# Wide attention: values behind the ring on TensorE, exponentials behind the ring copies on ScalarE

## The chip, the cores and the metric

The kernel runs on one core of a Trainium2 chip. The metric is the device time of one execution in microseconds (us); several runs give a median. The core has a matrix engine (TensorE, PE in the profile, its weight loads PEld), a vector engine (VectorE, DVE), a scalar engine (ScalarE, ACT), GpSimd (POOL) and an engine that mostly issues DMAs (SyncE, SP). Each works through its own instructions strictly in the order in which they are written; only semaphores tie one engine to another.

## What is computed

The whole program is a decoder of four layers with attention, cross attention and feed forward parts. The change touches one part, the cross attention of layer 1, over 8 batch entries, 256 queries each, and a context of 1601 rows with one learned null row added (1602 keys), 16 heads of 64:

```python
q = _split_heads(jnp.einsum('bnd,df->bnf', x, Wq))
kv = jnp.einsum('bmc,cf->bmf', context, Wkv)
k, v = jnp.split(kv, 2, axis=-1)
...
k = jnp.concatenate((nk, k), axis=-2)
v = jnp.concatenate((nv, v), axis=-2)
q = q * scale
sim = jnp.einsum('bhid,bhjd->bhij', q, k)
attn = jax.nn.softmax(sim, axis=-1)
out = jnp.einsum('bhij,bhjd->bhid', attn, v)
out = out.transpose(0, 2, 1, 3).reshape(b, -1, INNER)
out = jnp.einsum('bnf,fd->bnd', out, Wout)
```

A layer norm follows. All of it is float32.

## The kernel before

The stage (`stage4`) works in **units**: a unit is one batch entry and a pair of heads, 64 units in all. The two heads of a unit lie in the upper and the lower 64 partitions, so their score matmuls use the two halves of TensorE's rows, and their value matmuls the two halves of its columns. The 1602 keys of a unit are cut into 13 tiles of up to 128 (the last has 66), the tiles into 7 **slots** (six of two tiles, the last of one). The main loop of every engine takes two slots in a **step**. Since a unit has 7 slots, the pattern repeats after 14 slots, which are seven steps and two units.

A slot x passes these stations:

- scores (TensorE, L2870): keys by queries into one of two pairs of PSUM banks, keys on the partitions;
- score copy (ScalarE, L2942): PSUM to the SBUF tile `sc`;
- maxima (VectorE, L3027 and L3030): a running elementwise maximum over the tiles of the unit;
- ten slots later (`LAG - 2`) the subtraction of the maximum in place (VectorE, L3008) and the exponential in place (ScalarE, L2948); GpSimd adds the exponentials up tile by tile (L2992);
- twelve slots later (`LAG`) the values (TensorE, L2884), accumulated over the unit in PSUM;
- fourteen slots after the last slot of a unit the **sums** (TensorE, L2925: ones times the added exponentials), then on VectorE the reciprocal (L3040) and the multiplication (L3043).

Between these, TensorE does what the following units need, in a **ring** of two PSUM banks. `ring_of(s)` lists the keys of a step in their order: `q` (L2837), `k` in four chunks (L2846) and `v` (L2854) are projections; `turn` (L2904) transposes the maxima of a unit, whose reduce over keys VectorE makes (L3016); `bcast` (L2911) spreads the result over the partitions; `out` (L2919) is the output projection, once in 8 units. A key can start only when the key two places before it has been copied out of its bank (`ring_bank`, which waits for `n - 2`). The copies are ScalarE's (L2958 for q, L2964 for k, L2970 for v, L2975 for bcast), that of `turn` is VectorE's reduce and that of `out` a VectorE copy.

The order by hand in a step is, before the change:

- TensorE: scores, values, ring, sums;
- ScalarE: score copies, exponentials, ring copies;
- VectorE (unchanged): subtractions, reduce of a turn, maxima, copy of `out`, reciprocal and multiplication;
- GpSimd (unchanged): the adds.

A turn of unit u-1 is in the step with slot 7u+1, the sums of a unit in the step with a slot 7m-1, so the step with sums is followed at once by a step with a turn. The scores of a new unit wait for the copies of its q and of its last k chunk. The values of a step wait for exponentials that ScalarE made in the step before.

Of the kernel before, what the change touches and what calls it, by code (L numbers as in the profile page):

```python
# [16 lines left out]
ACT = mybir.ActivationFunctionType  # L17
# [2756 lines left out]
def stage4(env):  # L2774
    ps, branch, x_feat, ident = env.ps, env.branch, env.x_feat, env.ident
    with ExitStack() as ctx:
        st = Stage(env, ctx, "wide")
        plan = WideSlots()
# [46 lines left out]
        @block.tensor  # L2825
        def _(pe):
            def ring_bank(key):
                n = plan.index[key]
                if n >= 2:
                    wait_copied(pe, plan.order[n - 2])  # L2830
                return n % 2

            def project(key):
                if key[0] == "q":
                    u = key[1]
                    bank = ring_bank(key)
                    return pe.matmul(ps[:, bank, 0:S], W("wq")[:, u % HP * P:u % HP * P + P],  # L2837
                                     x_feat[:, u // HP * S:u // HP * S + S], start=True, stop=True)
                if key[0] == "k":
                    u, c = key[1:]  # L2840
                    if u % HP == 0 and c == 0:
                        pe.wait_ge(ctx_loaded, 16 * (u // HP + 1))
                    bank = ring_bank(key)
                    lo, hi = plan.chunks[c]
                    for half in range(2):
                        ins = pe.matmul(ps[:, bank, 0:hi - lo],  # L2846
                                        W("wk")[:, half * INNER + u % HP * P:half * INNER + u % HP * P + P],
                                        ctxT[:, u // HP % 2, half, lo:hi], start=(half == 0), stop=(half == 1))
                    return ins
                g, t = key[1:]  # L2850
                bank = ring_bank(key)
                c0, rows = t * P, min(P, SC - t * P)
                for half in range(2):
                    ins = pe.matmul(ps[0:rows, bank, 0:2 * P], ctxT[:, g // 4 % 2, half, c0:c0 + rows],  # L2854
                                    W("wv")[:, half * INNER + g % 4 * 2 * P:half * INNER + g % 4 * 2 * P + 2 * P],
                                    start=(half == 0), stop=(half == 1))
                return ins

            def scores(s, u, k):
                if k == 0:  # L2860
                    wait_copied(pe, ("q", u))
                    wait_copied(pe, ("k", u, 3))
                if s >= 2:
                    pe.wait_ge(s_copied, s - 1)
                    before, step = plan.unit(s, 2)
                    pe.wait_ge(max_done, len(tiles) * before + plan.tiles_of(step)[-1] + 1)
                for t in plan.tiles_of(k):
                    c0, rows = tiles[t]
                    for e in range(2):
                        ins = pe.matmul(ps[0:rows, 2 + 2 * (s % 2) + e, t % 2 * S:(t % 2 + 1) * S],  # L2870
                                        kT[e * HW:(e + 1) * HW, u % 2, c0:c0 + rows],
                                        q[e * HW:(e + 1) * HW, u % 2, :], start=True, stop=True)
                ins.then_inc(st_ready, 1)

            def values(s, u, k):
                if k == 0 and u >= 2:
                    pe.wait_ge(normed, u - 1)
                wait_copied(pe, ("v", u // 2, plan.tiles_of(k)[-1]))
                pe.wait_ge(exp_done, s + 1)
                for t in plan.tiles_of(k):  # L2880
                    rows = tiles[t][1]
                    for e in range(2):
                        c0 = u % 2 * P + e * HW
                        ins = pe.matmul(ps[e * HW:(e + 1) * HW, 6 + u % 2, 0:S], v[0:rows, u // 2 % 2, t, c0:c0 + HW],  # L2884
                                        sc[0:rows, u % 2, t, e * S:(e + 1) * S], start=(t == 0), stop=(t == last_tile))
                ins.then_inc(pv_done, 1)

            pe.wait_ge(w_loaded, 16)
            pe.wait_ge(null_moved, 32)
            pe.wait_ge(null_k_ready, 1)  # L2890
            pe.wait_ge(ones_ready, 1)
            for s in range(plan.first, plan.end, 2):
                for slot in plan.pair(s):
                    scores(*slot)
                for slot in plan.pair(s, plan.LAG):
                    values(*slot)
                for key in plan.ring_of(s):
                    if key[0] in ("q", "k", "v"):
                        project(key).then_inc(ring_ready, 1)
                    elif key[0] == "turn":  # L2900
                        pe.wait_ge(max_done, len(tiles) * (key[1] + 1))
                        bank = ring_bank(key)
                        for j in range(4):
                            ins = pe.transpose(ps[:, bank, j * P:(j + 1) * P], top[:, key[1] % 2, j * P:(j + 1) * P],  # L2904
                                               ident[:, :])
                        ins.then_inc(ring_ready, 1)
                    elif key[0] == "bcast":
                        wait_copied(pe, ("turn", key[1]))
                        bank = ring_bank(key)
                        for j in range(4):  # L2910
                            ins = pe.matmul(ps[:, bank, j * P:(j + 1) * P], mx[:, j:j + 1].to_broadcast([P, P]),  # L2911
                                            ident[:, :], start=True, stop=True)
                        ins.then_inc(ring_ready, 1)
                    else:
                        pe.wait_ge(normed, HP * (key[1] + 1))
                        bank = ring_bank(key)
                        for qt in range(2):
                            for p in range(HP):
                                ins = pe.matmul(ps[:, bank, qt * D:(qt + 1) * D], oT[:, p, qt * P:(qt + 1) * P],  # L2919
                                                W("wout")[:, p * D:(p + 1) * D], start=(p == 0), stop=(p == HP - 1))  # L2920
                        ins.then_inc(ring_ready, 1)
                for u in plan.ended(s, plan.LAG + 2):
                    pe.wait_ge(added, last_tile * (u + 1))
                    for e in range(2):
                        ins = pe.matmul(ps[e * HW:(e + 1) * HW, 6 + u % 2, S:2 * S], ones[:, :],  # L2925
                                        acc[:, u % 2, e * S:(e + 1) * S], start=True, stop=True)
                    ins.then_inc(sums_done, 1)

        @block.scalar
        def _(act):  # L2930
            act.wait_ge(null_moved, 32)
            for s in range(plan.first, plan.end, 2):
                for x, u, k in plan.pair(s):
# [6 lines left out]
                    src = ps[0:rows, 2 + 2 * (x % 2):4 + 2 * (x % 2), 0:n * S].rearrange("p e (j q) -> p e j q", j=n)  # L2940
                    dst = sc[0:rows, u % 2, 2 * k:2 * k + n, :].rearrange("p j (e q) -> p e j q", e=2)
                    act.activation(dst, src, ACT.Copy).then_inc(s_copied, 1)  # L2942
                for x, u, k in plan.pair(s, plan.LAG - 2):
                    n = len(plan.tiles_of(k))
                    rows = tiles[2 * k][1]
                    act.wait_ge(sub_done, x + 1)
                    e = sc[0:rows, u % 2, 2 * k:2 * k + n, :]
                    act.activation(e, e, ACT.Exp).then_inc(exp_done, 1)  # L2948
                for key in plan.ring_of(s):
                    if key not in plan.act_count:  # L2950
                        continue
# [7 lines left out]
                    elif key[0] == "k":  # L2959
                        u, c = key[1:]  # L2960
                        lo, hi = plan.chunks[c]
                        if u >= 2:
                            act.wait_ge(st_ready, plan.STEPS * (u - 1))
                        act.activation(kT[:, u % 2, lo:hi], ps[:, bank, 0:hi - lo], ACT.Copy).then_inc(ring_act, 1)  # L2964
                    elif key[0] == "v":
                        g, t = key[1:]
                        rows = min(P, SC - t * P)
                        if g >= 2:
                            act.wait_ge(pv_done, plan.STEPS * (2 * g - 3) + t // 2 + 1)
                        act.activation(v[0:rows, g % 2, t, :], ps[0:rows, bank, 0:2 * P], ACT.Copy).then_inc(ring_act, 1)  # L2970
                    else:
                        u = key[1]
                        if u >= 2:
                            act.wait_ge(sub_done, plan.STEPS * (u - 1))
                        act.activation(mb[:, u % 2, :], ps[:, bank, :], ACT.Copy).then_inc(ring_act, 1)  # L2975

        @block.gpsimd
        def _(pool):
# [1463 lines left out]
```

## Time and profile before

| | us |
|---|---|
| median of 3 runs | 5105.78 |
| lowest, highest | 5103.46, 5122.11 |
| the profiled execution, time | 5113.21 |
| the profiled execution, span of its trace | 5111.4 |
| TensorE busy, whole span | 4084.8 (80%) |
| VectorE, ScalarE, GpSimd busy | 3495.8, 2508.5, 1378.3 |

The stage lies from about 890 to 2708 us of the span. A row of a view by stretches reads: the stretch, its length, then the busy time (with the number of instructions) of PE, PEld, DVE, ACT and POOL, the clock granted to TensorE as a share of 2.4 GHz, the share of the DMA engines and GB/s. A row of the list of waits reads: who waited, for whom, the time in total, how often, the longest; all in us. A row of the timeline reads: start in us, busy time in us of the instructions that were merged into the row, engine, line, operation, output and input, shape, number; in brackets the idle time before it and who ended it. A matmul of float32 shows as two records, and a busy time in such a row runs to the end of the last matmul, which overlaps the next row; so the time that a group costs is read from start to start.

### The profile page before, as it was taken

The numbers are of one execution on the slowest core, as the hardware profiler recorded it, in microseconds if no ns is written. First come the engines' busy times: TensorE is split into PE (matmuls) and PEld (weight loads), VectorE is DVE, ScalarE is ACT, GpSimd is POOL, SyncE is SP. The second block draws the span as 40 slices with busy tenths as digits, with TensorE's granted clock in tenths as the row PEclk, the third lists the DMA queues.
The fourth block names the chain that finished last, engine by engine and source line by source line (L and its number), as shares of the span: only waits on it lengthen the run. The fifth ranks groups of instructions, "written<-read, shape, count | busy, mean of one in ns | idle before, by whom it ended". The sixth has DMA issues, their size and how long they took to land. (4 is left out here: it accounts for less than half of the span.)

```text
span 5111.4 us, 77588 instructions
## 1 busy us (share of the span) xinstructions
PE 4084.8 (80%) x29250; PEld 2216.5 (43%) x29315; DVE 3495.8 (68%) x5424; ACT 2508.5 (49%) x3542; POOL 1378.3 (27%) x1033
## 2 busy tenths in 40 slices
PE   5740596999999999999995995866995768888872
PEld 3530234666666666666652332432443332222221
DVE  5379444677777777777784445766773648888867
ACT  2120142666666666666662223543563345776762
POOL 0000300566666666666665302000000100000000
PEclk5565698999999999999997997987997788999986
DMA  0010001000000000000003106316540333323200
GB/s 19 1 60 0 0 0 51 1 14 1 14 1 14 14 1 14 1 14 1 1 1 129 58 0 148 54 14 108 81 72 4 95 66 59 55 43 49 47 2 8
DMA packets 135604, 167.70 MB, mean 33 GB/s; under 512 B 19499, under 2 KB 108093, under 8 KB 134677
## 3 DMA queue, kind: packets, MB, share of 16 engines
q1 hardware_dynamic: 127540, 146.39, 14.1%
q0 software_dynamic: 6528, 16.42, 1.3%
q8 instruction: 231, 3.78, 0.3%
q14 instruction: 121, 0.98, 0.1%
q10 hardware_dynamic: 1184, 0.12, 0.0%
HBM read 125.31 MB, written 34.55 MB: 31 GB/s over the span
## 5 line engine op out<-in xcount | busy, mean ns | idle before, releaser
L2992 POOL TENSOR_TENSOR arena<-arena 128x512 f32<-128x512 f32 (+1 forms) x768 | 1131.8, 1475 | 692.2 <-ACT arena L2948 638.8
L2443 ACT ACTIVATE arena<-ps 128x1024 f32<-128x1024 f32 (+1 forms) x688 | 703.9, 1024 | 331.9 <-PE ps L2368 321.4
L2461 DVE TENSOR_REDUCE arena<-ps 128x2 f32<-128x826 f32 (+1 forms) x576 | 565.0, 981 | 183.6 <-PE ps L2314 175.1
L3008 DVE TENSOR_TENSOR arena<-arena 128x1024 f32<-128x1024 f32 (+1 forms) x448 | 645.9, 1480 | 13.8 <-ACT arena L2975 13.8
L3030 DVE TENSOR_TENSOR arena<-ps,arena 128x512 f32<-128x512 f32 (+1 forms) x768 | 530.3, 691 | 177.8 <-ACT arena L2942 144.4
L2314 PE MATMUL ps<-arena 48*128 48x413 bf16 (+3 forms) x1920 | 435.2, 333 | 135.0 <-DVE arena L2461 67.2
L2942 ACT ACTIVATE arena<-ps 128x1024 f32<-128x1024 f32 (+1 forms) x448 | 410.6, 961 | 204.8 <-PE ps L2870 194.3
L2854 PE MATMUL ps<-arena 128*128 128x256 f32 (+1 forms) x1664 | 444.1, 392 | 20.5 <-DVE arena L3016 19.2
L2948 ACT ACTIVATE arena<-arena 128x1024 f32<-128x1024 f32 (+1 forms) x448 | 424.9, 992 | 50.7 <-DVE arena L3008 48.2
L2387 PE MATMUL ps<-arena 128*9 128x256 f32 (+2 forms) x5504 | 435.3, 388 | 11.7 <-ACT arena L2431 8.0
L2870 PE MATMUL ps<-arena 64*128 64x256 f32 (+1 forms) x3328 | 427.3, 391 | 5.6 <-ACT arena L2964 1.3
L2884 PE MATMUL ps<-arena 128*64 128x256 f32 (+1 forms) x3328 | 412.7, 388 | 5.8 <-ACT arena L2948 5.8
L2846 PE MATMUL ps<-arena 128*128 128x400 f32 (+1 forms) x1024 | 400.1, 513 | 2.9 <-ACT arena L2970 2.8
L2870 PEld LDWEIGHTS ps<-arena 64*128 64x128 f32 (+1 forms) x3328 | 301.1, 182 | 149.7 <-issue 94.8
L2368 PE MATMUL ps<-arena 51*128 51x256 bf16 (+3 forms) x2752 | 349.1, 276 | 10.5 <-DMA arena<-arena 10.5
L2854 PEld LDWEIGHTS ps<-arena 128*128 128x128 f32 (+1 forms) x1664 | 282.4, 185 | 154.5 <-issue 61.4
L2314 PEld LDWEIGHTS ps<-arena 48*128 48x128 bf16 (+1 forms) x1920 | 127.5, 96 | 461.1 <-DVE arena L2461 230.4
L2884 PEld LDWEIGHTS ps<-arena 128*64 128x64 f32 (+1 forms) x3328 | 220.7, 137 | 171.5 <-issue 84.5
L2262 POOL COPY arena<-arena 128x1536 f32<-128x1536 f32 (+2 forms) x40 | 30.0, 782 | 932.2 <-DMA arena<-arena 605.5
L2964 ACT ACTIVATE arena<-ps 128x400 f32<-128x400 f32 (+1 forms) x256 | 129.5, 506 | 256.7 <-PE ps L2846 256.7
L2846 PEld LDWEIGHTS ps<-arena 128*128 128x128 f32 x1024 | 182.6, 190 | 127.1 <-ACT arena L2970 14.3
L2368 PEld LDWEIGHTS ps<-arena 51*128 51x128 bf16 (+3 forms) x2752 | 170.4, 98 | 108.1 <-issue 55.0
(645 smaller groups left out, 5796.0 us busy)
## 6 DMA issues: line engine op xcount, KB each, us to landing
arena<-ctx_parts SPq DMA_DIRECT2D x96, 200.1 KB
arena<-ctx_parts SPq DMA_DIRECT2D x192, 100.1 KB
arena<-in_ctx_feat SPq DMA_DIRECT2D x8, 1601.0 KB, 6.5
arena<-in_ctx SPq DMA_DIRECT2D x16, 768.0 KB
arena<-diff_att_stack SPq DMA_DIRECT2D x60, 192.0 KB
ctx_parts<-arena SPq DMA_DIRECT2D x24, 400.2 KB, 3.7
arena<-in_w SPq DMA_DIRECT2D x1, 6416.0 KB, 18.6
arena<-in_ctx_feat SPq DMA_DIRECT2D x8, 800.5 KB
```

The source lines that it names most:

```text
L2314: return pe.matmul(self.ps[:, bank, c0:c0 + hi - lo], self.qst[r0:r1, ring, self.slot(g, h), q * P:(q + 1) * P], self.kst[r0:r1, ring, sel ...
L2368: ins = pe.matmul(self.ps[0:rows, 2 * (u % 2) + k % 2, k // 2 * S:(k // 2 + 1) * S], self.kst[r0:r1, ring, self.slot(g, k), c:c + rows], s ...
L2387: ins = pe.matmul(self.ps[32 * k:32 * k + self.hd + 1, 6, 0:S], self.vh[0:rows, b % 2, t, h0 + k, :], self.prob[0:rows, u % 3, k % 2 * 2 * ...
L2443: act.activation(self.prob[0:rows, u % 3, :], self.ps[0:rows, 2 * (u % 2):2 * (u % 2) + 2, :].rearrange("p n c -> p (n c)"), ACT.Exp).then ...
L2461: ins = dve.tensor_reduce(dst[:, :, j // 2], self.ps[:, 4:6, 0:hi - lo], AX.X, ALU.max)
L2846: ins = pe.matmul(ps[:, bank, 0:hi - lo], W("wk")[:, half * INNER + u % HP * P:half * INNER + u % HP * P + P], ctxT[:, u // HP % 2, half, ...
L2854: ins = pe.matmul(ps[0:rows, bank, 0:2 * P], ctxT[:, g // 4 % 2, half, c0:c0 + rows], W("wv")[:, half * INNER + g % 4 * 2 * P:half * INNER ...
L2870: ins = pe.matmul(ps[0:rows, 2 + 2 * (s % 2) + e, t % 2 * S:(t % 2 + 1) * S], kT[e * HW:(e + 1) * HW, u % 2, c0:c0 + rows], q[e * HW:(e + ...
L2884: ins = pe.matmul(ps[e * HW:(e + 1) * HW, 6 + u % 2, 0:S], v[0:rows, u // 2 % 2, t, c0:c0 + HW], sc[0:rows, u % 2, t, e * S:(e + 1) * S], ...
L2992: pool.tensor_tensor(acc[0:rows, u % 2, :], before, sc[0:rows, u % 2, t, :], ALU.add).then_inc(added, 1)
L3008: dve.tensor_tensor(e, e, mb[0:rows, u % 2, None, :].to_broadcast([rows, n, 2 * S]), ALU.subtract).then_inc(sub_done, 1)
L3030: ins = dve.tensor_tensor(most, got, most, ALU.max)
```

## The change

Two blocks move; nothing is added or removed, and no wait is changed. In TensorE's step `values` goes from between the scores and the ring to behind the ring, ahead of the sums. In ScalarE's step the exponentials go from between the score copies and the ring copies to the end.

```diff
             for s in range(plan.first, plan.end, 2):
                 for slot in plan.pair(s):
                     scores(*slot)
-                for slot in plan.pair(s, plan.LAG):
-                    values(*slot)
                 for key in plan.ring_of(s):
...
                         ins.then_inc(ring_ready, 1)
+                for slot in plan.pair(s, plan.LAG):
+                    values(*slot)
                 for u in plan.ended(s, plan.LAG + 2):
                     pe.wait_ge(added, last_tile * (u + 1))
...
                     act.activation(dst, src, ACT.Copy).then_inc(s_copied, 1)
-                for x, u, k in plan.pair(s, plan.LAG - 2):
-                    n = len(plan.tiles_of(k))
-                    rows = tiles[2 * k][1]
-                    act.wait_ge(sub_done, x + 1)
-                    e = sc[0:rows, u % 2, 2 * k:2 * k + n, :]
-                    act.activation(e, e, ACT.Exp).then_inc(exp_done, 1)
                 for key in plan.ring_of(s):
...
                         act.activation(mb[:, u % 2, :], ps[:, bank, :], ACT.Copy).then_inc(ring_act, 1)
+                for x, u, k in plan.pair(s, plan.LAG - 2):
+                    n = len(plan.tiles_of(k))
+                    rows = tiles[2 * k][1]
+                    act.wait_ge(sub_done, x + 1)
+                    e = sc[0:rows, u % 2, 2 * k:2 * k + n, :]
+                    act.activation(e, e, ACT.Exp).then_inc(exp_done, 1)
```

TensorE, in the step with a turn that follows a step with sums (the row L2925), before the change. Line numbers behind the moved block differ by two after it: L2904 becomes L2902, L2911 becomes L2909.

```order
L2925 MATMUL ps<-arena 64x256 x2
L2870 MATMUL ps<-arena 128x256 x8
L2884 MATMUL ps<-arena 64x256 x8
L2904 MATMUL ps<-ident,arena 128x128 x4
L2837 MATMUL ps<-x_feat,arena 128x256
L2854 MATMUL ps<-arena 128x256 x2
L2911 MATMUL ps<-ident,arena 128x128 x4
L2854 MATMUL ps<-arena 128x256 x2
L2846 MATMUL ps<-arena 128x401 x2
L2870 MATMUL ps<-arena 128x256 x8
```

The same place on TensorE after the change:

```order
L2884 MATMUL ps<-arena 64x256 x8
L2925 MATMUL ps<-arena 64x256 x2
L2870 MATMUL ps<-arena 128x256 x8
L2902 MATMUL ps<-ident,arena 128x128 x4
L2837 MATMUL ps<-x_feat,arena 128x256
L2854 MATMUL ps<-arena 128x256 x2
L2909 MATMUL ps<-ident,arena 128x128 x4
L2854 MATMUL ps<-arena 128x256 x2
L2846 MATMUL ps<-arena 128x401 x2
L2884 MATMUL ps<-arena 64x256 x8
L2870 MATMUL ps<-arena 128x256 x8
```

The values (L2884) have left the place between the scores (L2870) and the turn and stand at the end of the step; in the step before they now stand next to the sums (L2925).

ScalarE, in the same two steps, before the change:

```order
L2942 ACTIVATE arena<-ps 66x512
L2948 ACTIVATE arena<-arena 128x1024 x2
L2970 ACTIVATE arena<-ps 65x256
L2964 ACTIVATE arena<-ps 128x400
L2942 ACTIVATE arena<-ps 128x2x2x256 x2
L2948 ACTIVATE arena<-arena 128x1024 x2
L2958 ACTIVATE arena<-ps 128x256
```

ScalarE at the same place after the change (the exponential is L2975 now, the copy of v L2964, of k L2958, of q L2952):

```order
L2942 ACTIVATE arena<-ps 66x512
L2964 ACTIVATE arena<-ps 65x256
L2958 ACTIVATE arena<-ps 128x400
L2975 ACTIVATE arena<-arena 128x1024 x2
L2942 ACTIVATE arena<-ps 128x2x2x256 x2
L2952 ACTIVATE arena<-ps 128x256
```

The two exponentials have moved behind the copies of v and k of their step.

## Rows read from the trace of the kernel before

**Rows 1.** Busy times by stretch, middle of the stage.

```profile
1600.00:1800.00 200.00, 196.89 (x1202) 126.34 (x1198) 153.74 (x165) 128.69 (x190) 126.32 (x86) 1.00 0.03 9
```

**Rows 2.** List of waits, 880 to 2700 us.

```profile
PEld ps L2870 <- ACT arena L2964: 32.6, 64, 1.3
...
PE ps L2854 <- DVE arena L3016: 19.2, 32, 0.6
...
PEld ps L2846 <- ACT arena L2970: 14.3, 31, 3.2
```

**Rows 3.** Timeline of TensorE, steps G (from 1765.83) and A (from 1772.27).

```profile
1765.83 1.57 PE L2870 MATMUL ps<-arena 64*128 64x256 f32 x12
...
1771.56 0.65 PE L2925 MATMUL ps<-arena 128*64 128x256 f32 x4
1772.27 2.00 PE L2870 MATMUL ps<-arena 64*128 64x256 f32 x16
1774.19 1.95 PE L2884 MATMUL ps<-arena 128*64 128x256 f32 x16
1776.07 0.66 PE L2904 MATMUL ps<-ident,arena 128*128 128x128 f32 x4
...
1777.79 1.13 PE L2854 MATMUL ps<-arena 128*128 128x256 f32 x4 [0.63 <-DVE arena L3016]
...
1782.05 2.00 PE L2870 MATMUL ps<-arena 64*128 64x256 f32 x16
```

**Rows 4.** Timeline of TensorE, sums and then step E (from 1748.91).

```profile
1748.33 0.65 PE L2925 MATMUL ps<-arena 128*64 128x256 f32 x4
...
1748.91 2.00 PE L2870 MATMUL ps<-arena 64*128 64x256 f32 x16
...
1752.72 0.66 PE L2904 MATMUL ps<-ident,arena 128*128 128x128 f32 x4
...
1753.21 1.03 PE L2854 MATMUL ps<-arena 128*128 128x256 f32 x4
...
1754.25 1.58 PE L2846 MATMUL ps<-arena 128*128 128x401 f32 x4
...
1758.95 1.35 PE L2870 MATMUL ps<-arena 64*128 64x256 f32 x10
```

**Rows 5.** Timeline of VectorE, steps A and E, and other pairs of subtractions.

```profile
1751.16 1.84 DVE L3008 TENSOR_TENSOR arena<-arena 128x1024 f32<-128x1024 f32 x2
...
1757.39 2.43 DVE L3008 TENSOR_TENSOR arena<-arena 128x1024 f32<-128x1024 f32 x2 [0.44 <-ACT arena L2975]
...
1764.05 3.62 DVE L3008 TENSOR_TENSOR arena<-arena 128x1024 f32<-128x1024 f32 x2
...
1772.26 1.76 DVE L3040 RECIPROCAL arena<-ps 128x256 f32<-128x256 f32 x1 [1.98 <-PE ps L2925]
...
1774.39 2.75 DVE L3008 TENSOR_TENSOR arena<-arena 128x1024 f32<-128x1024 f32 x2
1777.06 0.68 DVE L3016 TENSOR_REDUCE arena<-ps 128x4 f32<-128x512 f32 x1
```

**Rows 6.** Timeline of ScalarE and GpSimd in step G.

```profile
1768.41 2.00 ACT L2948 ACTIVATE arena<-arena 128x1024 f32<-128x1024 f32 x2
...
1771.66 0.51 ACT L2964 ACTIVATE arena<-ps 128x400 f32<-128x400 f32 x1 [0.96 <-PE ps L2846]
...
1769.54 5.38 POOL L2992 TENSOR_TENSOR arena<-arena 128x512 f32<-128x512 f32 x4 [0.72 <-ACT arena L2948]
```

**Rows 7.** Stretches and timeline of TensorE, start and end of the stage.

```profile
926.00:927.00 1.00, 0.68 (x1) 0.50 (x2) 1.00 (x1) 0.55 (x3) 0.99 (x1) 0.50 0.00 0
...
926.33 3.04 PE L2846 MATMUL ps<-arena 128*128 128x400 f32 x4 [2.83 <-ACT arena L2970]
...
2669.60 2.08 PE L2911 MATMUL ps<-ident,arena 128*128 128x128 f32 x8 [4.88 <-DVE arena L3016]
...
2666.80:2673.60 6.80, 4.00 (x18) 3.03 (x20) 5.25 (x5) 3.23 (x4) 4.33 (x4) 0.50 0.01 2
```

## The prediction

> **What bounds the kernel now.** The change touches one stage of the program, the wide attention, so I looked first at the busy times by stretch. In 1600 to 1800 us TensorE is busy 196.89 of 200 us at a granted clock of 1.00, VectorE 153.7, ScalarE 128.7 and GpSimd 126.3 [rows 1]. TensorE is the bound, the others have 23 to 37% of slack, and any time in which TensorE waits is added to the kernel. Next I read the list of waits. TensorE waits for VectorE's reduce L3016 32 times, 19.2 us in all; the weight loads of the scores stand 32.6 us for the last key copy of a unit (L2964), 64 times, and 14.3 us for a value copy (L2970) [rows 2]. That is all there is to win: 0.3 to 0.5 us at a time.
>
> Then the timeline. The order of work repeats every 14 slots (two units, seven steps): 55.1 us. The two steps that hold a "turn" decide the case; I call them A and E. The reader should lay the rows of TensorE and of VectorE side by side.
>
> Step A begins with the scores at 1772.27. Scores take 1.92 us, values 1.88, then come the turn (1776.07), q and, at 1777.79, a v projection that had to wait 0.63 us for VectorE's reduce; the next step begins at 1782.05, so A lasts 9.78 us [rows 3]. Why is the reduce late? VectorE starts the reciprocal at 1772.26, because the sums of the step before were issued only at 1771.56, then the multiplication, then two subtractions (1774.39, 2.75 us), and only then the reduce at 1777.06 [rows 3, 5]. The reduce is tied to the sums and not to the turn: VectorE takes its work in order. With two ring banks, the second projection behind the turn can't start until the reduce has emptied the turn's bank.
>
> Step E begins at 1748.91: turn at +3.81 us, v at +4.30, k at +5.34, next step at +10.04 [rows 4]. VectorE's subtractions start at +2.25 and take 1.84 us [rows 5].
>
> **What the change moves.** It adds and removes no instruction; it costs only through order. (1) TensorE's values go from between scores and ring to behind the ring. (2) ScalarE's exponentials go from between score copies and ring copies to behind the ring copies.
>
> (1) In A and E the 1.9 us of values lay under VectorE's chain from reciprocal to reduce. That cover is taken away; the sums stay the last thing before the next scores, so the chain keeps its place. Queued behind TensorE's new wait are the rest of the ring, the values and all that follows; ScalarE's ring copies wait with it.
>
> (2) The exponentials end later in the step. Values use the exponentials of the step before, so these still have some 5 us; no wait there. But GpSimd adds what the exponentials deliver. In step G (before A) the exponentials run at 1768.41 and GpSimd's four adds at 1769.54 for 5.38 us, done at 1774.92, just as A's subtractions begin [rows 6]. G starts at 1765.83 [rows 3]. Its key copy stood at 1771.66 for 0.51 us [rows 6]; without the values (1.88) ahead of the projection it comes at 1769.8, and the exponentials follow it at 1770.3, 4.5 us into G instead of 2.6. The adds start 1.1 us after them, as now, at 5.6 of the 6.2 us that G then takes. GpSimd then works from A's start to A +5.4 or later, over the whole of A's subtractions. The same shift puts the adds of the step before E over E's.
>
> What subtractions cost beside GpSimd is in the trace: a pair takes 2.43 us with GpSimd idle (1757.39) and 3.62 us beside its adds (1764.05) [rows 5]. For A I take 3.62 for 2.75. E's pair is one full and one half tile: 3.62/2 for the full one and about 1.2 for the half one, an estimate, 3.0 for 1.84. Lower bound for both: as now.
>
> In the Trainium skill, "SBUF — State Buffer", section "SBUF: two separate sides", the port pair that VectorE and GpSimd share is an exclusive lock and the loser blocks for a whole instruction. By that rule each subtraction could wait out one add (5.38/4 = 1.35 us), a pair taking 2.43 + 2.7 = 5.1 us; the trace's pair beside adds took 3.62 [rows 5], so the measurement decides and the rule stays a rival.
>
> **Step A after.** Scores no longer wait for the key copy, so sums to scores is 0.58 (1748.33 to 1748.91, [rows 4]) instead of 0.71 (1771.56 to 1772.27, [rows 3]), and all of VectorE's chain shifts to +0.12: subtractions at 2.25, reduce at 2.25 + 3.62 - 0.08 = 5.79, v 0.73 later (as 1777.06 to 1777.79) at 6.52. TensorE is free at 1.93 + 0.5 (turn) + 0.5 (q, an estimate by the turn's) = 2.93: 3.6 us idle. From v to the end of A took 4.26 us; to this the values come: 6.52 + 4.26 + 1.93 = 12.71, against 9.78: **+2.93 us**.
>
> **Step E after.** Reduce ends at 2.25 + 3.0 + 0.6, k at 5.9; TensorE is free at 1.93 + 0.49 + 1.0 = 3.4: 2.5 us idle. k to the end took 4.70 (1754.25 to 1758.95): 5.9 + 4.70 + 1.93 = 12.5, against 10.04: **+2.5 us**. If subtractions stay as fast as now, A is +2.06 and E +1.43.
>
> **What comes back.** The last key copy of a unit is now under the values (two a period, 0.3 us each net of the change of tiling that stays), and a ring copy no longer stands behind two exponentials (0.2). Sum: **-0.7 us**. By [rows 2] it can't exceed (32.6 + 14.3)/31 = 1.5. The other steps have no new wait.
>
> Per period: 2.93 + 2.5 - 0.7 = +4.7 us. The reciprocal precedes the turn in 31 periods: **+147 us**.
>
> **The clock.** TensorE never idled in mid-stage; now it would idle 3.6 and 2.5 us per period. What follows such idling is in the same stage at its start: after 2.83 us of idle time the granted clock is 0.50 (926 to 927 us), which is 1.2 instead of 2.4 GHz, and the four matmuls of a k projection show 3.04 us where they show 1.58 at 1754.25 [rows 4, 7]: 1.4 us lost. At the stage's end the very chain of this prediction stands bare: few values left to cover the reduce, 4.88 us of idle time until 2669.60, and the clock at 0.50 for 6.8 us, 2666.8 to 2673.6 [rows 7]. So a fall costs from 1.4 us to half of 6.8, 3.4 us. For A I take 1.7 (nearest to the first row, a little more since its idle time is longer), for E 1.5 in two falls of three: 1.0. Together 2.7 x 31 = **+84 us**. Bounds: 0, and 2 x 3.4 x 31 = 211.
>
> On this the Trainium skill ("TensorE: Matmul & The Clock Gate", section "HAM oscillation — how this bites in real kernels") tells of a kernel whose matmuls restarted at half clock after each recurring wait. By that rule the 84 us belong in the sum; without it the sum would be 147. The rows at 926 us and 2667 us agree with it.
>
> One thing is won once: the wait at 926.33 stood behind the first exponentials and goes, 2.83 + 1.4 = 4 us.
>
> Sum: 147 + 84 - 4 = +227 us. The profiled execution had a span of 5111.4 us and took 5113.21; 5113 + 227 = 5340. It lies 7 us above the median of the runs (5105.78), so the forecast for the median is 5106 + 227 = **5333 us**, 4.4% slower.
>
> **The rivals.**
> - The clock holds. For it: most of the stage runs at 1.00 with small gaps. Against: both long gaps of this stage brought it down. 5106 + 147 - 4 = 5249. Chance 0.18.
> - GpSimd's adds don't fall on the subtractions. A +2.06, E +1.43, less 0.7: 2.79 x 31 = 86; with 1.4 us for a fall in A alone, 43 more: 5188 to 5231. Chance 0.09.
> - Half clock for the long spell, as at 2666.8, in both steps: 2 x (3.4 - 0.5 of idle time in it) = 5.8 instead of 2.7 a period: 5333 + 96 = 5429. Chance 0.05.
> - Subtractions blocked for a whole add each: 1.5 us more in A and as much in E, x 31 = 93: 5426. The rule is that of "SBUF — State Buffer" in the Trainium skill. Chance 0.03.
> - Faster. The mechanism is the key copy: scores of a new unit find it ready. Price -0.7 us a period, 22 us, and 4 at the start: 5080. It decides only if the reduce has ended by +2.9 us in A and +3.4 in E, when TensorE wants the bank; but the reciprocal (1.76 us) and the subtractions alone reach past +4. Chance 0.04.
> - Nothing within the noise: TensorE's losses met by gains, up to 1.5 us a period and half of A's loss. Chance 0.02.
>
> **How the numbers follow.** The forecast has 0.59. Its own range, with the bounds of the clock term and shorter subtractions, is 5270 to 5400. To hold 8 in 10 the range takes in the held clock and the upper end of the second rival: 5210 to 5400. Slower than by 0.5% (26 us, about what a measurement of this kernel can tell from no change) are all but the last two: 0.94; within 0.02; faster 0.04.
>
> **What would show it.** Waits of TensorE for the reduce should go from 19 us to some (3.6 + 2.5) x 31 = 190 us, 62 to 64 times; if they stay under 60 us the account of the cover is wrong. The wait of the scores for L2964's successor goes. A pair of subtractions behind a reciprocal lasts 3 us or more; if 2.4 to 2.8, the second rival holds. The granted clock of 1000 to 2600 us falls from 1.00 to some 0.9; if it stays, the first rival does. The stage's period goes from 55.1 to some 62.5 us. I would be wrong altogether if VectorE got its reciprocal done earlier, or if ScalarE's later exponentials held TensorE's values, which I price at nothing: cover is 5 us, and a step would lose what exceeds it.

## The result: 5.6% slower

| | median, us | runs | lowest to highest |
|---|---|---|---|
| before | 5104.62 | 4 | 5088.74 to 5122.11 |
| changed | 5394.40 | 4 | 5391.39 to 5399.71 |

The ratio is 1.0563, with a 95% interval of 1.054 to 1.0586: 290 us more. 5333 us were forecast, 61 us too little; the time lies inside the range (5210 to 5400), some 6 us below its upper end. The profiled execution of the changed kernel has a span of 5394.8 us, 283.4 more than before.

Where the time went is seen best in the list of waits of TensorE in the stage (880 to 2990 us; it ends later now). Columns as in [rows 2]; the reduce of a turn is still L3016, the key copy is L2958 now.

```profile
PE ps L2854 <- DVE arena L3016: 132.5, 32, 4.3
PE ps L2846 <- DVE arena L3016: 98.2, 30, 3.4
...
PEld ps L2870 <- ACT arena L2958: 2.8, 3, 1.3
```

TensorE waits 230.7 us for the reduce, 62 times, where [rows 2] had 19.2 us, 32 times. The wait of the scores for the last key copy, 32.6 us in [rows 2], has gone to 2.8. The second thing is the clock, in the busy times by stretch, whose counterpart is [rows 1]:

```profile
1600.00:1800.00 200.00, 177.09 (x1032) 117.81 (x1029) 128.96 (x141) 108.96 (x162) 100.35 (x73) 0.93 0.03 9
944.00:2938.00 1994.00, 1763.62 (x10212) 1167.87 (x10211) 1296.31 (x1411) 1091.85 (x1614) 1018.98 (x733) 0.93 0.02 6
```

TensorE is busy 177 of 200 us instead of 197, and the granted clock is 0.93 instead of 1.00. With the two levels 1.0 and 0.5 (2.4 and 1.2 GHz) that is 14% of the 1994 us at half clock, some 280 us by the rounded figure.

A step A of the changed kernel, TensorE and then VectorE, against [rows 3] and [rows 5]:

```profile
1707.27 0.60 PE L2925 MATMUL ps<-arena 128*64 128x256 f32 x4
1707.80 2.00 PE L2870 MATMUL ps<-arena 64*128 64x256 f32 x16
1709.73 0.66 PE L2902 MATMUL ps<-ident,arena 128*128 128x128 f32 x4
1710.22 0.60 PE L2837 MATMUL ps<-x_feat,arena 128*128 128x256 f32 x2
1715.09 2.07 PE L2854 MATMUL ps<-arena 128*128 128x256 f32 x4 [4.28 <-DVE arena L3016]
1716.96 1.92 PE L2909 MATMUL ps<-ident,arena 128*128 128x128 f32 x8
...
1722.18 1.95 PE L2884 MATMUL ps<-arena 128*64 128x256 f32 x16
1724.06 2.00 PE L2870 MATMUL ps<-arena 64*128 64x256 f32 x16
```

```profile
1707.91 1.76 DVE L3040 RECIPROCAL arena<-ps 128x256 f32<-128x256 f32 x1 [1.84 <-PE ps L2925]
1709.71 0.42 DVE L3043 TENSOR_TENSOR arena<-ps,arena 128x256 f32<-128x256 f32 x1
1710.05 4.39 DVE L3008 TENSOR_TENSOR arena<-arena 128x1024 f32<-128x1024 f32 x2
1714.36 0.68 DVE L3016 TENSOR_REDUCE arena<-ps 128x4 f32<-128x512 f32 x1
```

The step starts at 1707.80, so VectorE's reciprocal starts at +0.11, the subtractions at +2.25, the reduce at +6.56 and TensorE's v projection at +7.29. The first two came as forecast to 0.01 us; the reduce was forecast for +5.79 and v for +6.52. The difference is the pair of subtractions: 4.39 us, not 3.62. Behind the wait TensorE is at half clock: the turn's broadcast (L2909) shows 1.92 us, where [rows 7] had 2.08 at half clock. From v to the values (1722.18) it takes 7.09 us, where the prediction had 4.26 at full clock; the whole step takes 16.26 us. GpSimd works beside the subtractions, and the exponentials that feed it stand late in step G, which starts at 1701.64:

```profile
1706.00 1.99 ACT L2975 ACTIVATE arena<-arena 128x1024 f32<-128x1024 f32 x2
...
1707.12 6.23 POOL L2992 TENSOR_TENSOR arena<-arena 128x512 f32<-128x512 f32 x4 [0.80 <-ACT arena L2975]
```

Exponentials +4.4 us into G, adds from +5.5 on and until 1713.35, over all but the last microsecond of the subtractions; in [rows 6] the adds had ended at 1774.92, half a microsecond into them.

Taken one by one, the same subtractions and adds show what makes the pair long. First those of the step above, then the pair at 1764.05 of the kernel before, from which the prediction had its 3.62 us:

```profile
1709.89 1.27 POOL L2992 TENSOR_TENSOR arena<-arena 128x512 f32<-128x512 f32 x1
1710.05 2.19 DVE L3008 TENSOR_TENSOR arena<-arena 128x1024 f32<-128x1024 f32 x1
1711.23 2.12 POOL L2992 TENSOR_TENSOR arena<-arena 128x512 f32<-128x512 f32 x1
1712.16 2.28 DVE L3008 TENSOR_TENSOR arena<-arena 128x1024 f32<-128x1024 f32 x1
```

```profile
1763.09 1.28 POOL L2992 TENSOR_TENSOR arena<-arena 128x512 f32<-128x512 f32 x1 [5.50 <-ACT arena L2948]
1764.05 1.41 DVE L3008 TENSOR_TENSOR arena<-arena 128x1024 f32<-128x1024 f32 x1
1764.52 2.07 POOL L2992 TENSOR_TENSOR arena<-arena 128x512 f32<-128x512 f32 x1
1765.38 2.29 DVE L3008 TENSOR_TENSOR arena<-arena 128x1024 f32<-128x1024 f32 x1
```

A subtraction takes 1.2 us when no add runs, an add 1.27. In both lists each instruction that begins while the other engine is at work ends 1.1 us (1.08 to 1.13) after the other one's end: 1711.16 and 1712.24, 1713.35, 1714.44; 1764.37 and 1765.46, 1766.59, 1767.67. The two engines take turns, and a record that is longer than 1.3 us holds the wait for the other. So a pair costs more the earlier in an add it begins. At 1764.05 the add had 0.32 us left, at 1710.05 it had 1.11; the difference is 0.79 us, and 4.39 - 3.62 = 0.77.

### The profile page after: what moved, and what is told of

The parts are those of the page before. It is cut to its first block and busy times, and to the rows that moved or that the text cites. A ratio compares the mean times of both kernels' runs of the same rounds, so it can differ in the third digit from the quotient of the medians.

```text
span 5394.8 us, 77653 instructions
## 1 busy us (share of the span) xinstructions
PE 4178.2 (77%) x29315; PEld 2310.5 (43%) x29315; DVE 3478.4 (64%) x5424; ACT 2500.7 (46%) x3542; POOL 1321.5 (24%) x1033
## 5 line engine op out<-in xcount | busy, mean ns | idle before, releaser
L2992 POOL TENSOR_TENSOR arena<-arena 128x512 f32<-128x512 f32 (+1 forms) x768 | 1074.8, 1401 | 1041.4 <-ACT arena L2975 983.1
L2443 ACT ACTIVATE arena<-ps 128x1024 f32<-128x1024 f32 (+1 forms) x688 | 703.9, 1024 | 323.5 <-PE ps L2368 312.9
L3030 DVE TENSOR_TENSOR arena<-ps,arena 128x512 f32<-128x512 f32 (+1 forms) x768 | 530.2, 690 | 469.1 <-ACT arena L2942 435.7
L3008 DVE TENSOR_TENSOR arena<-arena 128x1024 f32<-128x1024 f32 (+1 forms) x448 | 631.7, 1445 | 77.5 <-ACT arena L2969 77.5
L2854 PE MATMUL ps<-arena 128*128 128x256 f32 (+1 forms) x1664 | 496.0, 428 | 133.8 <-DVE arena L3016 132.5
L2846 PE MATMUL ps<-arena 128*128 128x400 f32 (+1 forms) x1024 | 422.2, 537 | 98.2 <-DVE arena L3016 98.2
L2854 PEld LDWEIGHTS ps<-arena 128*128 128x128 f32 (+1 forms) x1664 | 313.5, 205 | 268.4 <-DVE arena L3016 145.4
L2975 ACT ACTIVATE arena<-arena 128x1024 f32<-128x1024 f32 (+1 forms) x448 | 419.3, 986 | 9.4 <-DVE arena L3008 9.2
L2870 PE MATMUL ps<-arena 64*128 64x256 f32 (+1 forms) x3328 | 418.5, 389 | 1.4 <-ACT arena L2958 0.7
L2884 PE MATMUL ps<-arena 128*64 128x256 f32 (+1 forms) x3328 | 411.8, 388 | 4.1 <-ACT arena L2975 4.1
L2870 PEld LDWEIGHTS ps<-arena 64*128 64x128 f32 (+1 forms) x3328 | 296.6, 182 | 118.9 <-issue 86.1
L2884 PEld LDWEIGHTS ps<-arena 128*64 128x64 f32 (+1 forms) x3328 | 220.8, 137 | 202.8 <-issue 105.8
L2958 ACT ACTIVATE arena<-ps 128x400 f32<-128x400 f32 (+1 forms) x256 | 129.5, 506 | 383.8 <-PE ps L2846 383.8
L2964 ACT ACTIVATE arena<-ps 128x256 f32<-128x256 f32 (+1 forms) x416 | 159.7, 384 | 300.2 <-PE ps L2854 299.2
L2846 PEld LDWEIGHTS ps<-arena 128*128 128x128 f32 x1024 | 203.4, 206 | 219.2 <-DVE arena L3016 84.1
```

Source lines behind the costliest of these rows:

```text
L2443: act.activation(self.prob[0:rows, u % 3, :], self.ps[0:rows, 2 * (u % 2):2 * (u % 2) + 2, :].rearrange("p n c -> p (n c)"), ACT.Exp).then ...
L2846: ins = pe.matmul(ps[:, bank, 0:hi - lo], W("wk")[:, half * INNER + u % HP * P:half * INNER + u % HP * P + P], ctxT[:, u // HP % 2, half, ...
L2992: pool.tensor_tensor(acc[0:rows, u % 2, :], before, sc[0:rows, u % 2, t, :], ALU.add).then_inc(added, 1)
L3008: dve.tensor_tensor(e, e, mb[0:rows, u % 2, None, :].to_broadcast([rows, n, 2 * S]), ALU.subtract).then_inc(sub_done, 1)
L3030: ins = dve.tensor_tensor(most, got, most, ALU.max)
```

## The experiments

The theory in one line: the values had covered VectorE's chain reciprocal, multiplication, subtractions, reduce; uncovered, the chain holds up TensorE, GpSimd's adds make it longer, and the clock charges the idle time a second time. Rivals: the moved exponentials carry the loss; TensorE waits for something else; adds or clock are of no account. Each kernel was timed beside the kernel before on the same chip.

### The two halves, one at a time

TensorE's half alone:

```diff
                 for slot in plan.pair(s):
                     scores(*slot)
-                for slot in plan.pair(s, plan.LAG):
-                    values(*slot)
...
+                for slot in plan.pair(s, plan.LAG):
+                    values(*slot)
                 for u in plan.ended(s, plan.LAG + 2):
```

> The kernel before with TensorE's half of the change alone: values behind the ring; ScalarE keeps exponentials ahead of its ring copies. Theory (values covered VectorE's chain from reciprocal to reduce; GpSimd's adds lengthen the chain only where the exponentials moved too): subtractions behind a reciprocal stay at about 2.75 and 1.84 us, TensorE waits for the reduce 2.7 and 1.4 us per period, some 130 us in all; 5105 + 86 for the waits net of the gains + 40 to 60 for the clock = 5230 to 5250 us. Rival (the moved exponentials carry the loss, by way of GpSimd's adds): under 5150 us.

Measured: 5394.2 us, ratio 1.0554 (1.0527 to 1.058). That is as slow as the whole change, and 150 us above the expectation. The waits of TensorE show what had been left out of it:

```profile
PE ps L2854 <- ACT arena L2970: 98.1, 92, 1.8
PE ps L2854 <- DVE arena L3016: 86.2, 32, 2.8
PE ps L2846 <- ACT arena L2970: 45.2, 31, 2.8
PE ps L2846 <- DVE arena L3016: 38.7, 30, 1.4
```

The waits for the reduce are 125 us, as the theory had it (130); VectorE's pair behind a reciprocal was 2.89 and 1.81 us. But there are 143 us more, for ring copies (L2970). The ring now follows the scores at once, and ScalarE, in its old order, has two exponentials (2 us) ahead of the ring copies. Where the values have moved, ScalarE's half repairs this. It brings 106 us of waits for the reduce in exchange (230.7 against 125) and more time at half clock (0.93 against 0.98 over 1000 to 2600 us), so the two kernels come out at the same time by different ways.

ScalarE's half alone:

```diff
                     act.activation(dst, src, ACT.Copy).then_inc(s_copied, 1)
-                for x, u, k in plan.pair(s, plan.LAG - 2):
...
+                for x, u, k in plan.pair(s, plan.LAG - 2):
+                    n = len(plan.tiles_of(k))
```

> The kernel before with ScalarE's half alone: exponentials behind the ring copies; TensorE keeps values between scores and ring. Theory: GpSimd's adds now lie over the subtractions of the two steps with a turn, which take 4.4 and 3.8 us instead of 2.75 and 1.84 (as they do with the whole change); with the cover of the values in place 1.6 and 1.5 us of this reach TensorE per period, 95 us, and little of the clock: 5200 to 5230 us. Rival (the moved exponentials carry the loss by themselves): 5350 or more. Rival (contention is of no account): 5105.

Measured: 5149.58 us, ratio 1.0086 (1.0069 to 1.0103): +44 us, half of the expected loss. The mechanism is there but smaller: the pair of subtractions in a step A took 3.43 us (from 2.75), and TensorE waits 1.3 us there; in step E it waits 0.5 us.

```profile
PE ps L2854 <- DVE arena L3016: 40.1, 32, 1.3
PE ps L2846 <- DVE arena L3016: 14.6, 30, 0.6
...
1734.68 3.43 DVE L3008 TENSOR_TENSOR arena<-arena 128x1024 f32<-128x1024 f32 x2
```

I had taken the durations of the changed kernel (4.4 and 3.8 us) over to this one; here the adds run beside the whole pair too, but the first subtraction begins when the running add has only 0.08 us left, and the second alone waits out an add:

```profile
1733.48 1.28 POOL L2992 TENSOR_TENSOR arena<-arena 128x512 f32<-128x512 f32 x1 [1.98 <-ACT arena L2975]
1734.68 1.22 DVE L3008 TENSOR_TENSOR arena<-arena 128x1024 f32<-128x1024 f32 x1
1735.81 2.30 DVE L3008 TENSOR_TENSOR arena<-arena 128x1024 f32<-128x1024 f32 x1
```

Both rivals fall with this run: the exponentials alone don't carry the loss, and contention is of some account.

### The chain itself: the reduce ahead of the subtractions

In the changed kernel, on VectorE alone:

```diff
             for s in range(plan.first, plan.end, 2):
-                for x, u, k in plan.pair(s, plan.LAG - 2):
...
                 for key in plan.ring_of(s):
                     if key[0] == "turn":
...
                                           AX.X, ALU.max).then_inc(ring_dve, 1)
+                for x, u, k in plan.pair(s, plan.LAG - 2):
...
+                    dve.tensor_tensor(e, e, mb[0:rows, u % 2, None, :].to_broadcast([rows, n, 2 * S]), ALU.subtract
+                                      ).then_inc(sub_done, 1)
```

> The changed kernel, and on VectorE the reduce of a turn put ahead of the subtractions of its step. Theory (the loss is all in the chain reciprocal, multiplication, subtractions, reduce): the reduce ends at about +3.0 us of its step, just as TensorE has done turn and one projection; TensorE's waits for the reduce fall from 231 us to under 20, the clock stays at 1.00, and what is left is the gain of the change, 20 us and the 20 us of the old waits: 5060 to 5085 us. Rival (TensorE waits for other things by the new order, such as late exponentials or copies): well over 5105, up to 5390.

Measured: 5060.35 us, ratio 0.9913 (0.9896 to 0.9931): 334 us faster than the changed kernel and 45 us faster than the kernel before. The rows of a step A (start 1749.72), waits, and the clock (the reduce is L3008 here, the subtractions L3016):

```profile
1752.34 0.69 DVE L3008 TENSOR_REDUCE arena<-ps 128x4 f32<-128x512 f32 x1 [0.29 <-PE ps L2902]
1752.95 3.42 DVE L3016 TENSOR_TENSOR arena<-arena 128x1024 f32<-128x1024 f32 x2
...
PE ps L2854 <- DVE arena L3008: 10.8, 31, 0.4
...
1600.00:1800.00 200.00, 198.78 (x1231) 129.99 (x1231) 159.94 (x168) 131.33 (x195) 132.62 (x88) 1.00 0.03 9
```

The reduce is done at +3.3 us instead of +7.2; the subtractions are still long beside GpSimd (3.42 us) and hold nobody up. The whole loss was in this chain and in the clock that fell with its waits: with it gone nothing of the new order costs. This is also the version that beats both kernels.

The same edit on the kernel before:

> The kernel before, with the reduce of a turn ahead of the subtractions of its step; TensorE and ScalarE as before. Theory: the wait of 0.63 us per period for the reduce goes, 20 us: 5085. The difference to the changed kernel with the same edit is what the new order is worth by itself: 20 us by my sum. Rival (VectorE's reduce now makes it wait for the turn, which comes at +3.8 us, and its subtractions and maxima late): 5105 or more.

Measured: 5272.91 us, ratio 1.0328 (1.0311 to 1.0345). A gain of 20 us was expected, a loss of 168 came: the rival is right. What stands at the head of VectorE's step now waits for a turn that TensorE issues behind the values, at +3.8 us:

```profile
DVE arena L3008 <- PE ps L2904: 145.3, 63, 6.5
...
PE ps L2911 <- ACT arena L2958: 80.2, 31, 2.6
...
PE ps L2911 <- ACT arena L2970: 46.1, 31, 2.0
```

In a step E (from 1705.09) the subtractions start at 1710.20, +5.1 us instead of +2.25 [rows 4, 5], ScalarE waits for them with its exponentials, and the ring copies queued behind the exponentials come late for the broadcast (L2911): 126 us of waits, on an engine two stations away from the edit. The granted clock falls to 0.98 over 1000 to 2600 us, which is some 30 us more by an estimate (2% of 1600 us).

The last two combinations, TensorE's half and ScalarE's half, each with the reduce first:

> TensorE's half alone with VectorE's reduce ahead of the subtractions. With TensorE's half alone the trace showed a second wait beside that for the reduce (125 us): 143 us for copies of the ring (L2970) that stand behind exponentials on ScalarE. Theory: the edit on VectorE takes away the 125 us and leaves the 143 us or more, since the exponentials get later: 5200 to 5300 us; ScalarE's half is what makes the order good. Rival (the reduce was all): 5060.

Measured: 5432.24 us, ratio 1.0622 (1.0601 to 1.0643), the slowest of all; I had expected 5200 to 5300. The 143 us of waits for ring copies stayed, as expected; those for the reduce went down to 10.8 (L2854 for L3008), as expected; but the broadcast got the same 126 us of new waits as in the run above (L2909 for L2958 80.2, for L2970 46.0), which I had named ("or more") and not sized.

> ScalarE's half alone with VectorE's reduce ahead of the subtractions. The kernel before with the reduce first took 5273 us. Theory of that loss: VectorE waits for a turn that TensorE issues only behind the values, its subtractions and the exponentials come late, and the ring copies behind these hold TensorE (126 us in that trace). With the exponentials behind the ring copies this goes: 5100 to 5150 us. Rival (late subtractions hold TensorE by another way): near 5273.

Measured: 5139.48 us, ratio 1.0059 (1.0041 to 1.0077). With the exponentials behind the ring copies the loss of 168 us shrinks to 28, and no wait of a broadcast for a ring copy is left among the larger ones. So most of the loss of that edit went by way of the ring copies behind the exponentials, as the theory had it. What is left goes at least in part by another way: the scores now wait 27.4 us for VectorE's maxima (L3030), 64 times, which in the kernel before were 0.6 us.

All eight orders together, in us against the kernel before:

| | reduce behind subtractions | reduce first |
|---|---|---|
| neither moved | 0 | +168 |
| exponentials moved | +44 | +28 |
| values moved | +289 | +321 |
| both moved | +290 | -45 |

No edit of the three is good by itself, and no pair is; only when all three engines take first what the others wait for is there a gain.

### GpSimd's adds

The changed kernel, all adds but the first of a unit cut to 16 columns, so that most of the denominator is left out:

```diff
-                    pool.tensor_tensor(acc[0:rows, u % 2, :], before, sc[0:rows, u % 2, t, :], ALU.add).then_inc(added, 1)
...
+                        pool.tensor_tensor(acc[0:rows, u % 2, 0:16], acc[0:rows, u % 2, 0:16], sc[0:rows, u % 2, t, 0:16],
+                                           ALU.add).then_inc(added, 1)
```

> The changed kernel with GpSimd's adds cut to 16 of 512 columns, all but the first of each unit; it leaves out most of the softmax's denominator. Theory (GpSimd's adds, moved onto the subtractions by ScalarE's half, lengthen the chain): a pair of subtractions behind a reciprocal falls from 4.4 to 2.4 us and from 3.8 to 1.9 us, TensorE's waits for the reduce from 231 to about 120 us, as with TensorE's half alone, and the half-clock time with them: 5394 - 113 - 70 = about 5210 us. Rival (adds and subtractions don't meet): 5394.

Measured: 5177.12 us, ratio 1.0123 (1.0103 to 1.0143), 217 us less than the changed kernel (225 by the ratios to the kernel before). The subtractions in a step E and in a step A, and the waits for the reduce (L3020 in this kernel):

```profile
1729.07 1.81 DVE L3012 TENSOR_TENSOR arena<-arena 128x1024 f32<-128x1024 f32 x2
...
1753.20 2.35 DVE L3012 TENSOR_TENSOR arena<-arena 128x1024 f32<-128x1024 f32 x2
...
PE ps L2854 <- DVE arena L3020: 69.0, 32, 2.2
...
PE ps L2846 <- DVE arena L3020: 38.7, 30, 1.4
```

The pairs take 2.35 us in A and 1.81 in E, and the waits fall from 230.7 to 107.7. So more than half of the wait in the changed kernel is the adds on top of the subtractions. The other 94 us of the 217 I put down to the clock, which is 0.98 here and was 0.93 (1000 to 2600 us); 5% of 1600 us are 80, an estimate of the right size, but that share is argued, not measured.

### The clock

The changed kernel with spare matmuls where TensorE would idle, into the ring bank that has just been copied out; their result is overwritten:

```diff
+                    n = plan.index[key]
+                    if n >= 2 and plan.order[n - 2][0] == "turn" and plan.order[n - 2][1] >= 2:
+                        wait_copied(pe, plan.order[n - 1])
+                        for i in range(6):
+                            pe.matmul(ps[:, (n - 1) % 2, 0:S], W("wq")[:, 0:P], x_feat[:, 0:S], start=True, stop=True)
```

> The changed kernel with six spare matmuls of 256 columns (2.6 us) at the place where TensorE would wait for the reduce, into the ring bank that has just been copied out; nothing is left out. Theory (the idle time costs twice, the second time by the clock): idle time behind the turn falls by what the spare matmuls take, the chain and the step keep their length, the granted clock stays at 1.00, and the 118 us that half clock costs by the trace (236.5 us of busy time at 0.50) go: 5275 to 5290 us. Rival (half clock costs little, since VectorE's chain sets the pace anyway): 5394 or, if the spare matmuls are in the way, more.

Measured: 5292.85 us, ratio 1.0359 (1.0334 to 1.0383): 102 us less than the changed kernel (104 by the ratios), by adding work. The stage in the view by stretches, and the scores of a step E with the k projection that waited for the reduce:

```profile
944.00:2830.00 1886.00, 1826.90 (x10954) 1214.82 (x10952) 1294.07 (x1411) 1092.90 (x1616) 1020.38 (x733) 1.00 0.02 6
...
1707.78 2.00 PE L2870 MATMUL ps<-arena 64*128 64x256 f32 x16
...
1714.53 1.61 PE L2846 MATMUL ps<-arena 128*128 128x401 f32 x4
```

The clock stays at 1.00. The k projection starts at +6.75 us of its step E and takes 1.61 us; in the changed kernel it starts at +6.75 too (1755.92 in the step from 1749.17) and shows 3.04. So the spare matmuls leave the chain as it is, and what changes is the work behind the wait. What is left against the kernel before, some 185 us (181 on the same chip, 188 against the table above), is the chain at full clock; so of the 290 us some 100 are the clock. The expected gain was 105 to 120.

## Why the prediction was right, and 61 us short

**The cover.** Right. Chain and step A came out to 0.01 us up to the subtractions, the reduce first took the whole loss away, and the cover alone (adds short) costs 108 us of waits, near the 120 us of that run's expectation.

**GpSimd's adds.** The direction and the place were right: adds over the subtractions of A and E. The size was the term that was too small. I took 3.62 and 3.0 us from pairs in [rows 5] beside adds; the steps showed 4.39 and 3.84. The single rows above say why: the two engines take turns, and the pair of [rows 5] had begun near the end of an add, those of the changed kernel near its start. In the waits that is 230.7 us against the forecast 190 (3.6 + 2.5 us, 31 times): +41 us. The Trainium skill ("SBUF — State Buffer", section "SBUF: two separate sides") has the shared port pair as an exclusive lock that is held for a whole instruction, and the rows agree: in each list every instruction ends 1.1 us after the one of the other engine. I had set the rule aside for the measured 3.62 and left it a chance of 0.03. Its price of 5.1 us was too high, because it charged each subtraction a whole add of 1.35 us on top of its own time; the rows show 0.98 and 1.07 us (2.19 and 2.28 less 1.21). That the time lies inside the range all the same is owed in part to luck: the mechanism at work was one that I had nearly ruled out.

**The clock.** Right in kind; 84 us forecast, 102 measured by the spare matmuls. In the step A shown above the clock cost 2.8 us (7.09 from v to the values, for 4.26), where I had taken 1.7. That step is one of the worst: the next A, from 1778.23 to 1793.23, takes 15.0 us and not 16.26. By the run with the spare matmuls, the chain net of its gains came to 188 us for 143 and the clock to 102 for 84; together 63 us, where 61 were missing.

**What comes back.** 22 us and 4 at the start were forecast. With the reduce first the new order is 45 us faster than the kernel before (35 to 53 by the interval). The waits for the reduce went from 19.2 us [rows 2] to 10.8, which is 8 of it; some 37 remain, somewhat more than the 26 forecast. The terms of that sum, twice 0.3 and 0.2, make 0.8 us a period and not 0.7.

**Priced at nothing.** I held that the later exponentials cost TensorE nothing by waits, and the changed kernel bears that out (4.1 us in 2 waits, TensorE's values for L2975). What I had not seen is that they are needed there: without them TensorE's half waits 143 us for ring copies. In the prediction the gain from the ring copy stood as 0.2 us a period; it was never the gain of the second half but the condition of the first.

**The rivals.** The clock didn't hold; adds and subtractions met (in that rival's sum E is +1.34, 2.5 less the 1.16 of the subtractions, and not +1.43; it moves the rival by 3 us); the blocked subtractions were the right mechanism at too high a price; the faster rival had the right condition, a reduce that has ended by about +2.9 us: at +3.3 the kernel with the reduce first shows it, 20 us better than the 5080 worked out for it.

**What the profile was to show.** Waits of some 190 us, 62 to 64 times: 230.7, 62. A pair of 3 us or more: 4.39 and 3.84. Clock some 0.9: 0.93. The wait for the key copy gone: 2.8 us. A period of some 62.5 us was too short: from the step E at 1749.17 to the next, at 1814.71, it is 65.5, and with the spare matmuls 61.1 (1707.78 to 1768.87).

## What to carry to other kernels

Before work is moved off a place in an in-order queue, ask what ran under it on the other engines: here 1.9 us of matmuls covered a chain that never appeared as a wait of more than 0.6 us. When a step's order is turned on one engine, turn its partners too, so that each engine takes first what the others ask for first; single edits of such a set can all look bad (+290, +168, +44) while the set is a gain (-45). Price idle time of TensorE twice where gaps recur as long as here, 3.3 and 4.3 us: 102 of 290 us were the clock. And before work of GpSimd is moved beside work of VectorE, look at the single rows of both: how much of an add was left decided between 1.2 and 2.3 us for the same subtraction.

## What the runs showed of the hardware

A VectorE subtraction of two SBUF operands (128 x 1024, float32) took 1.2 us alone (2.35 for a pair, with short adds). Beside GpSimd's adds of two SBUF operands (128 x 512, 1.27 us alone) it took from 1.22 to 2.30 us, and the adds up to 2.12 in the rows shown: each ended 1.1 us after the other engine's instruction that was running when it began. So these two engines are tied by more than the semaphores that the opening section names.

TensorE's idle gaps of 1.3 us in each period (exponentials moved alone) left the clock at 1.00 over 1000 to 2600 us. With gaps of 2.2 and 1.3 us (short adds) it was 0.98, with gaps of 2.8 us and many of 0.5 to 1.8 (values moved alone) also 0.98, and with 4.3 and 3.3 us 0.93. A gap of one length didn't always have the same effect. In the changed kernel the k projection behind a gap of 3.3 us ran at half clock in one step E and at full clock in the next:

```profile
1755.92 3.04 PE L2846 MATMUL ps<-arena 128*128 128x401 f32 x4 [3.29 <-DVE arena L3016]
...
1821.45 1.61 PE L2846 MATMUL ps<-arena 128*128 128x401 f32 x4 [3.28 <-DVE arena L3016]
```

That matmuls whose result nobody reads make a kernel 102 us faster I had expected from the sum, but not seen before as plainly.
